# Eight heads instead of four in the attention loops' body of a two-layer graph network

## The reference

```python
# N = 3327 nodes, 128 features; D = 128 "heads", inner width H = 8
h = relu(layernorm(x));  x = x + (A/deg(A)) @ h @ W_in + (A.T/deg(A.T)) @ h @ W_out
h = relu(layernorm(x))
q = (h @ Wq.T).reshape(D, N, H)          # k and v likewise
a = einsum('dnh,dmh->dnm', q, k) * D**-0.5 + A + A
a = softmax(a, axis=2)
out = einsum('dnm,dmh->dnh', a, v).reshape(N, H*D) @ Wo.T
x = x + out
```

## Time and profile before

| | us |
|---|---|
| median of 3 runs | 10639.18 |
| lowest and highest of them | 10638.48, 10643.95 |
| the profiled execution | 10635.45 |
| its span, first to last instruction | 10633.6 |
| attention loops in it | 9814.6 |

### The profile page before, as it was taken

One profiled execution on the slowest core, in us unless ns is written; L12 is line 12 of the kernel. 1 busy time (PEld: TensorE's weight loads), 2 busy tenths in 40 slices (PEclk: granted clock), 3 DMA queues, 4 the chain that ended last, 5 costly groups with the idle time before them and its releaser, 6 DMA issues. The chain is left out here.

```text
span 10633.6 us, 541170 instructions
## 1 busy us (share of the span) xinstructions
PE 10364.3 (97%) x216961; PEld 6794.6 (64%) x216961; DVE 9501.0 (89%) x10333; ACT 10156.5 (96%) x7762; POOL 8414.0 (79%) x4247
## 2 busy tenths in 40 slices
PE   7979999999999999999999999999999999999998
PEld 6646666666666666666666666666666666666666
DVE  7669999999989999999998999999998999999997
ACT  4479999999999999999999999999999999999997
POOL 4468888888888888888887888888887888888885
PEclk9989999999999999999999999999999999999999
DMA  7671111111121111111112111111112111111113
GB/s 226 211 245 42 42 42 42 42 42 42 42 81 45 42 42 42 42 42 42 42 42 82 42 42 42 42 42 42 43 42 74 42 42 42 42 42 42 41 42 89
DMA packets 537408, 638.97 MB, mean 60 GB/s; under 512 B 166638, under 2 KB 477299, under 8 KB 532115
## 3 DMA queue, kind: packets, MB, share of 16 engines
q1 hardware_dynamic: 535570, 609.12, 20.6%
HBM read 477.50 MB, written 131.20 MB: 57 GB/s over the span
## 5 line engine op out<-in xcount | busy, mean ns | idle before, releaser
L1219 DVE SCALAR_TENSOR_TENSOR at_sum<-attention_adj_t,at_score 128x832 f32<-128x832 f32 x9216 | 8811.4, 1017 | 870.3 <-PE at_score L1161 793.6
L1141 POOL TENSOR_TENSOR at_single<-at_single,attention_adj_t 128x832 f32<-128x832 f32 x4096 | 8078.3, 1995 | 1776.8 <-ACT at_single L1236 1759.5
L1239 ACT ACTIVATE at_sum<-at_sum 128x2496 f32<-128x2496 f32 x3072 | 7371.4, 2400 | 12.0 <-DVE at_sum L1219 12.0
L1161 PE MATMUL at_score<-attention_q,attention_k 128*32 128x512 bf16 (+1 forms) x106496 | 7200.9, 347 | 159.6 <-SPq L1106 51.0
L1161 PEld LDWEIGHTS at_score<-attention_q,attention_k 128*32 128x32 bf16 x106496 | 3597.2, 144 | 2265.7 <-DVE at_sum L1219 749.9
L1177 PE MATMUL at_acc<-at_sum,attention_v 128*9 128x208 f32 x73728 | 4844.6, 339 | 2.1 <-issue 1.1
L1236 ACT ACTIVATE at_single<-at_score 128x832 f32<-128x832 f32 x4096 | 3730.5, 962 | 32.2 <-PE at_score L1161 30.4
L1177 PEld LDWEIGHTS at_acc<-at_sum,attention_v 128*9 128x9 f32 x73728 | 1880.3, 91 | 896.0 <-issue 3.4
L1177 PE MATMUL at_acc<-at_single,attention_v 128*9 128x208 f32 x32768 | 2153.5, 339 | 0.0
L1177 PEld LDWEIGHTS at_acc<-at_single,attention_v 128*9 128x9 f32 x32768 | 835.4, 91 | 402.5 <-issue 1.0
L258 POOL TENSOR_TENSOR layer_col_acc<-layer_col_acc,st_a_rows 128x3328 f32<-128x3328 f32 x26 | 189.0, 7269 | 182.0 <-DMA st_a_rows<-in_adj_dram 182.0
(11 more groups left out here) (126 smaller groups left out, 1212.2 us busy)
## 6 DMA issues: line engine op xcount, KB each, us to landing
attention_k<-k_parts_scratch SPq DMA_DIRECT2D x1536, 156.0 KB
attention_q<-q_parts_scratch SPq DMA_DIRECT2D x4608, 13.0 KB
attention_v<-v_scratch SPq DMA_DIRECT2D x512, 112.5 KB
adj_t_scratch<-layer_a_t SPq DMA_DIRECT2D x26, 1664.0 KB, 7.6
st_a_rows<-in_adj_dram SPq DMA_DIRECT2D x25, 1663.5 KB, 9.3
attended_scratch<-at_o SPq DMA_DIRECT2D x1920, 7.3 KB
attention_adj_t<-adj_t_scratch SPq DMA_DIRECT2D x12, 2080.0 KB, 14.0
q_parts_scratch<-pr_partsq SPq DMA_DIRECT2D x18, 1024.0 KB, 5.9
```

The costliest lines, as they stand in the source:

```text
L1141: pool.tensor_tensor(slot(n), slot(n), plan.adjacency(at, b, n), ALU.mult).then_inc(multiplied, 1)
L1161: last = pe.matmul(score[plan.buffer(n)][32 * t:32 * (t + 1), a:b], keys[:, 32 * t:32 * (t + 1)], q[k][:, a:b], start=True, stop=True, til ...
L1219: dve.scalar_tensor_tensor(out=slot(n), in0=plan.adjacency(at, b, n), scalar=2.0, in1=score[plan.buffer(n)][:, 0:NB], op0=ALU.mult, op1=AL ...
L1239: act.activation(sums[buffer][:], sums[buffer][:], ACT.Exp).then_inc(exped, 1)
```

## The change

The body of all attention loops holds eight heads. A body then has 208 steps, one more than a multiple of three, so two irregular steps are needed to come out even: they lie at step 33 and at step 137 of the body, which is the eighth step (step 7, counted from 0) of the second and of the sixth head. There is still one irregular step for every four heads. The loops make half as many passes (63 on PE and ACT, 16 in each of the four loops of DVE and POOL).

```diff
@@ -48,7 +48,7 @@
 SINGLES = 8
-GROUP = 4
+GROUP = 8
 CHUNKS_AT_ONCE = 5
@@ -924,7 +924,7 @@
     EARLY = 3
-    TURN = C + 1
+    TURNS = (C + 7, 5 * C + 7)
@@ -987,7 +987,7 @@
         n %= self.n
-        return (n + (n >= self.TURN)) % SCORES
+        return (n + sum(n >= turn for turn in self.TURNS)) % SCORES
```

## The result

| | before | after |
|---|---|---|
| median, us | 10641.01 (4 runs) | 10797.08 (4 runs) |
| lowest to highest | 10638.48 to 10643.95 | 10793.70 to 10797.57 |
| ratio, 95% interval | | 1.0148 [1.0136, 1.0161] |
| profiled execution | 10635.45 | 10796.82 |

The change costs 156 us. The forecast was 10760 with a range of 10620 to 10835: the direction and the range hold, and the time is 37 us above the number. Two of its terms are off by more than that, in opposite directions.

The account below looks back on a forecast made before the run. ACT's exponentials bound the attention loops. A net loss of 2.0 us at 60 DVE branches, 120 us, on 10635.45 gave 10755; with 3.7 from profiled execution to median 10759, said as 10760, range 10620 to 10835.

Parts of the forecast that it names:

- What bounds the kernel, and by how much it could gain: Attention loops: ACT's exponentials take 19.08 us a head, 9769 of 9814.6 us, so at most about 46 us can return.
- DVE's fetch: DVE's branch back: the longer loop is fetched anew each pass, 3.4 us at each of 60 taken branches; chance 0.58.
- The cover of 0.60 us: Start of a body: ACT's slack against a late score, 0.41 + 0.19 us, taken off DVE's lateness of 2.4.
- PE's branch: PE's branch back, felt at step 12: half as many, visible part 9 to about 5 us; about 0.35 each without cover.
- Step 33: New irregular step: score 34 waits for step 32's addition, 0 to 0.4 us, 0.25 taken; step 137 costs nothing.
- The wait ahead of products 29 and 133: Old places of the irregular steps: ACT would no longer wait there; two old irregular steps cost 0.26 us for eight heads.
- The sum: Eight heads: 2.4 us lost less 0.4 of today's losses, net 2.0, at 60 taken DVE branches: 120 us.
- Its likeliest range: Whole kernel, if DVE fetches at every branch: a fetch of 3.2 to 4.6 us, giving 10740 to 10835 us.
- That the longer loop is kept: Rival at DVE's branch: no fetch, branch stays at 56 ns, around 9 us better, 10630; chance 0.24.
- That DVE's store holds five pieces and half the branches stall: Rival: two of DVE's four loops touch four pieces, two touch five; 30 x 2.2 us, 10696; chance 0.06.
- That ACT stalls too: Rival at ACT's branch: a loop over 256 instructions is fetched, 2.7 us lost 63 times, 10890; chance 0.08.

Follow-up runs that it names:

- the loop of 327 instructions: The kernel before with 104 more instructions (signals to a spare semaphore) in each of DVE's four loop bodies: 10742.01 against 10637.73 us, ratio 1.0099.
- one shift: The changed kernel with 130 more instructions on PE ahead of its loop: 10807.87 us, ratio 1.0159 against the kernel before.

## Why the prediction was right or wrong

**What bounds the kernel, and by how much it could gain.** Right. ACT's pace did not change, and all that went is in its losses at the ends of bodies.

**DVE's fetch.** The choice on which the forecast hung was right: q14 carries five or six packets for each body, DVE stands still at all 60 taken branches, and ACT waits for a score there. Its two sizes were off or right as follows. The fetch was put at 3.4 us by the earlier trace rows, with 3.2 as the lower end; it is 2.8, outside that. DVE's addition then starts 3.05 behind the branch in place of 1.3, 1.8 late where 2.4 was expected. The cover of 0.60 us came out right: 1.8 less 0.60 is 1.2, and the ledger has 1.14. So this term is 60 x 1.14 = 68 us, not 108.

**PE's branch.** Here the sum failed. It says that PE saves 64 branches and their visible part falls from 9 to 5 us, and that with cover gone each costs 0.35. The cost is 1.59 in the median, 102 us over the run. The 0.35 took over the branch's length of today, 692 ns. The prediction had noticed that PE's body is fetched anew at every pass, and did not ask whether the moment of the fetch of the branch's target, and so the branch's length, depends on how many instructions the body has. The earlier trace rows showed a branch ten times as long as those of the earlier trace rows, so that it contained a fetch could have been read there; that its length would change with the body could not, though a bound from above was at hand in the 3.74 us of PE's branch in the earlier trace rows, and it was not used. Two runs settle it: PE's loop at eight heads costs 59 us by itself, and 52 instructions in the body take these away. The branch ends some 2.5 us behind the start of the last packet, and with the new length of the body that packet starts 0.22 us ahead of it in place of 1.76. About 0.6 us of the 2.37 is DVE's stall ahead.

**Step 33.** Right: 0.25 was taken, 0.25 is the median at product 8 of the second head, and 2.4 us in all in the sixth, put at nothing. The wait ahead of products 29 and 133 is gone, as said.

**The sum.** By body, the prediction had 1.8 + 0.35 + 0.25 - 0.4 = 2.0. Measured: 1.14 + 1.59 + 0.25 - 0.4 = 2.6, times 60 is 155. An overestimate of 0.66 hid half of an underestimate of 1.24, so that the number came out as near as it did is in part luck: with the measured cost of the fetch and the rest as predicted, the sum is 1.34 x 60 = 80 us, or 10720. Its likeliest range also has a slip: by 6 us for each 0.1 us, a fetch of 3.2 gives 10748, not 10740.

**The rivals.** That the longer loop is kept fell: q14 has 375 packets. That DVE's store holds five pieces and half the branches stall fell in the changed kernel, but this pattern of two blocks out of four is just what the loop of 327 instructions shows, one piece lower. That ACT stalls too fell here, since its loop of 287 instructions stays within the four pieces, and it came true at 539 (sixteen heads). The branch was 45 ns, as before.

**What stays open.** DVE's stall makes the PE branch behind it longer by shortening the packet's lead (0.22 against 0.74, 1.10 against 1.91). Why the lead shrinks is not shown: PE catches up after the stall and so may reach the branch sooner behind the packet's start, but this was argued, not tested. The account of PE's lead rests on four lengths and one shift; no length between 80 and 132 beyond whole pieces was run, and the lead does not grow evenly with the length.

## What to carry to other kernels

Before a loop's body is lengthened, count its instructions for each engine: on DVE and ACT the pieces of 128 that it touches and the one behind must be four at most. By that rule up to some 256 are safe wherever the loop stands and up to 384 where it happens to stand well (the runs have 231, 287 and 327 kept); beyond that each pass stands still for 2.4 to 3.1 us at its branch, of which ACT here lost 1.1 to 1.5 for each branch. Engines need not have the same body: here 16 heads on PE and four on DVE are clearly better than eight for both, and better by 0.1% than four for both, with an interval that ends at 0.9999. For an engine whose loop is far too long to be kept, look at how far ahead of the branch the last packet of instructions starts; here 52 idle instructions were worth 64 us.

## What the runs showed of the hardware

The length of the branch instruction in the profile has a median of 56 ns on DVE before and of 63 after, 74 at most in both, whether it stalls or not; the 2.8 us show only as a gap to the next instruction, which the waits put down to PE. On PE the fetch is inside the branch's own duration. DVE's first packet starts 1.0 us behind the branch in the median of the changed kernel's stalls, and DVE goes on 1.8 behind the packet's start. PE's branch ends 2.4 to 2.6 us behind the start of its last packet, in the medians of all kernels.

Instructions come in packets of 16 KB (256 instructions) for PE and of 8.2 KB (128) for DVE and ACT. Two loops with the same instructions can differ by some 2.5 us a pass for where they stand (0.27 against 2.75 to 3.07 in the kernel with 327 instructions). For PE the place in memory did not matter (2312 against 2374 ns after a shift by half a piece), but the length of the body did (1814 against 748 ns for 52 instructions more).
